# Attention and experts in one kernel: the start's order re-laid, and a dense ring of six units with a lag of five

## What is computed

```python
x = x + tanh(g_xattn) * attended(layernorm(x), ctx)   # q = ln(x) Wq + bq, k = ctx Wk + bk, v = ctx Wv + bv
h = relu(einsum('bsd,edh->ebsh', layernorm(x), W1) + b1)          # 8 experts, 512 hidden
expert_out = einsum('ebsh,ehd->ebsd', h, W2) + b2
x = x + tanh(g_ffn) * einsum('bse,ebsd->bsd', top2_weights, expert_out)
```

## Time and profile before

| | us |
|---|---|
| three runs of the kernel | 282.55, 282.98, 285.04 (median 282.98) |
| the profiled execution | 281.82 |
| its span in the profile | 280.1 |
| TensorE busy in the span | 268.3 |
| VectorE busy | 210.6 |
| ScalarE busy | 186.6 |
| GpSimd busy | 109.6 |

### The profile page before, as it was taken

The page is one execution under the profiler, slowest core; times in us unless marked ns, Lnnn a source line. Parts: engine busy times, 40 slices in busy tenths (PEclk is TensorE's granted clock), DMA queues, the critical chain, the costliest instruction groups (busy, mean ns, idle before and its releaser), DMA issues.

```text
span 280.1 us, 5068 instructions
## 1 busy us (share of the span) xinstructions
PE 268.3 (96%) x1662; PEld 246.6 (88%) x1662; DVE 210.6 (75%) x406; ACT 186.6 (67%) x338; POOL 109.6 (39%) x144
## 2 busy tenths in 40 slices
PE   7899999999999999999999999989999999994994
PEld 6678999999999999999899999978989989993994
DVE  4889977995686997898456688667797895643796
ACT  3996565446566556556579888797457557965891
POOL 3899993556600030000006346710153434375130
PEclk9999999999999999999999999999999999999898
DMA  6700020000199000000000342443011112141112
GB/s 199 255 2 0 4 76 0 2 1 2 42 292 276 1 2 0 0 4 1 0 2 4 84 140 63 148 148 103 19 32 28 30 30 67 49 114 28 60 47 84
DMA packets 18485, 17.08 MB, mean 61 GB/s; under 512 B 2410, under 2 KB 14940, under 8 KB 18460
## 3 DMA queue, kind: packets, MB, share of 16 engines
q1 hardware_dynamic: 17372, 15.31, 18.0%
q0 software_dynamic: 640, 1.31, 1.6%
q10 hardware_dynamic: 448, 0.14, 0.2%
HBM read 13.34 MB, written 3.42 MB: 60 GB/s over the span
## 4 chain that ended last, share of the span: by engine, by line
PE 84%; DVE 8%; issue 4%; DMA 2%; ACT 1%; SPq 1%; DVEq 0%; another core or an unknown queue 0%; ACTq 0%
PE ps L1448 8%; PE ps L1474 8%; PE ps L1449 8%; PE ps L1476 8%; PE ps L1475 8%; PE ps L1450 7%; PE ps L1370 7%; PE ps L1575 4%; PE ps L1561 3%; PE ps L1602 2%; DVE pmax L975 2%; PE ps L1641 2%; PE ps L1600 2%; PE ps L1643 2%; PE ps L1642 2%
## 5 line engine op out<-in xcount | busy, mean ns | idle before, releaser
L882 ACT ACTIVATE ex_hi<-ps 128x768 fp32r<-128x768 f32 (+1 forms) x78 | 56.9, 730 | 57.7 <-PE ps L1450 54.4
L1190 DVE TENSOR_TENSOR ex_lo<-ps,ex_hi 128x768 fp32r<-128x768 f32 (+1 forms) x66 | 58.5, 886 | 24.5 <-ACT ps L886 18.8
L975 DVE TENSOR_REDUCE pmax<-ps 128x1 f32<-128x512 f32 (+2 forms) x74 | 62.4, 875 | 10.2 <-PE ps L1370 9.5
L1474 PE MATMUL ps<-ex_hi,ctx_both 128*97 128x384 f32 (+1 forms) x153 | 49.8, 325 | 0.0
L886 ACT ACTIVATE ps<-ps 128x768 f32<-128x768 f32 (+1 forms) x66 | 49.7, 752 | 0.0
L1449 PE MATMUL ps<-q_lo,ctxT_hi 96*128 96x384 f32 (+1 forms) x153 | 49.1, 321 | 0.0
L1450 PE MATMUL ps<-q_hi,ctxT_lo 96*128 96x384 f32 (+1 forms) x153 | 48.7, 318 | 0.0
L1476 PE MATMUL ps<-ex_lo,ctx_both 128*97 128x384 f32 (+1 forms) x153 | 48.6, 318 | 0.0
L1475 PE MATMUL ps<-ex_hi,ctx_both 128*96 128x384 f32 (+1 forms) x153 | 48.6, 318 | 0.0
L1448 PE MATMUL ps<-q_hi,ctxT_hi 97*128 97x384 f32 (+1 forms) x126 | 42.6, 338 | 1.5 <-DVE ex_lo L1190 1.4
L1370 PE MATMUL ps<-ctxT_hi,q_hi 97*128 97x512 f32 (+1 forms) x104 | 34.3, 400 | 0.6 <-DVE pmax L975 0.4
(11 more groups left out here) (227 smaller groups left out, 547.3 us busy)
## 6 DMA issues: line engine op xcount, KB each, us to landing
raw<-in_ctx_dram SPq DMA_DIRECT2D x6, 384.0 KB, 6.4
w_raw<-in_L_ffn_W_dram SPq DMA_DIRECT2D x8, 256.0 KB, 3.9
raw<-in_L_ffn_W_dram SPq DMA_DIRECT2D x8, 256.0 KB, 6.3
raw<-in_L_ffn_b_dram SPq DMA_DIRECT2D x8, 256.0 KB
shared<-routing SPq DMA_DIRECT2D x8, 192.0 KB
x_slots<-shared SPq DMA_DIRECT2D x1, 1088.0 KB, 6.3
y_slots<-shared SPq DMA_DIRECT2D x17, 64.0 KB, 1.5
shared<-in_L_ffn_b_dram SPq DMA_DIRECT2D x1, 512.0 KB, 3.8
```

The lines of the kernel that those rows point to most:

```text
L882: nc.scalar.activation(ex_pair(ex_hi, u % P_RING, js, n), scores, ACT.Exp)
L975: nc.vector.tensor_reduce(pmax[:, FIRST_TILE[ROUND_BLOCK[r]] + t, place:place + 1], max_home(s)[:, 0:w], AX.X, ALU.max).then_inc(max_reduc ...
L1190: nc.vector.tensor_tensor(ex_pair(ex_lo, u % P_RING, js, n), whole, ex_pair(ex_hi, u % P_RING, js, n).bitcast(F32), ALU.subtract).then_inc ...
L1474: nc.tensor.matmul(dst[0:CA, :], ch[:, j, :], hi, start=(j == first), stop=False)
```

## The change

It does these things:

- Ahead of block 0, TensorE's order becomes pass, window, pass, window: pass s is followed by window s + 2. Six of the multiplications of ident with ident are left out.
- x of block 1 is no longer turned in the start. It is turned at unit 6, its queries are made at unit 8 and split at unit 9; for block 2 these are units 15, 17 and 18. A wait on rows_copied is added ahead of block 2's, since both now use the last PSUM bank.
- VectorE makes the statistics of blocks 1 and 2 at units 3 and 10, and GpSimd's power and normalizing for them move behind the split of window 6 and behind all splits of the context.
- One pass moves from unit 10 to unit 14.
- H_LAG becomes 5 and H_RING 6, with two more PSUM banks (7 and 6) and six places in the buffers, and the waits that these need. scale_output of an expert moves two units back, to the second unit of the expert after next, and the transposes of the sum move to the last rounds of the loop.

```diff
-H_LAG = 3
-H_RING = 4
+H_LAG = 5
+H_RING = 6
-WARM_NORM = 6
-    FIRST_BLOCK_PASSES = [0, 1, 1, 0, 1, 1, 1, 1, 1, 1, 1, 0, 1, 1, 1, 2, 2, 2, 2, 2, 2, 2, 2, 1, 0, 0]
+    FIRST_BLOCK_PASSES = [0, 1, 1, 0, 1, 1, 1, 1, 1, 1, 0, 0, 1, 1, 2, 2, 2, 2, 2, 2, 2, 2, 2, 1, 0, 0]
-        QK_UNIT = {1: 1, 2: 8}
-        TURN_X_UNIT = {2: 6}
-        SPLIT_UNIT = {1: 2, 2: 9}
+        QK_UNIT = {1: 8, 2: 17}
+        TURN_X_UNIT = {1: 6, 2: 15}
+        STATISTICS_UNIT = {1: 3, 2: 10}
+        SPLIT_UNIT = {1: 9, 2: 18}
-            return [UB[0], ps[:, TURNED_BY_VECTOR % 4, :], UB[1]][b]
+            return UB[1] if b else UB[0]
-            return ps[:, [3, 2, 1, 0][u % 4], :]
+            return ps[:, [3, 2, 1, 0, 7, 6][u % H_RING], :]
-        HID_AT = [2 * H, 2 * H + SPAN, 2 * H + 2 * SPAN, H]
+        HID_AT = [SPAN * k for k in (3, 4, 5, 2, 1, 0)]
...
-            inverse_deviation(1)
-            normalize(1)
...
-            inverse_deviation(2)
-            normalize(2)
             for w in range(4, 7):
                 split_ctxT(w)
+            inverse_deviation(1)
+            normalize(1)
             split_ctx(2)
...
             for g in range(3, NG):
                 split_ctx(g)
+            inverse_deviation(2)
+            normalize(2)
...
-            copy_x(1)
...
-                elif u == H_RING - 1:
-                    act.wait_ge(ys_made, SLOT_TILES - 1)
+                elif u >= 3:
+                    act.wait_ge(ys_made, SLOT_TILES)
...
-            dve.wait_ge(x_later_in, 16)
-            statistics(0, 1)
-            statistics(0, 2)
...
+                    for later, unit in STATISTICS_UNIT.items():
+                        if b == 0 and i == unit:
+                            dve.wait_ge(x_later_in, 16)
+                            statistics(0, later)
...
-                if u == FU - 1:
-                    scale_output(e - 1)
-                if u % HC == H_LAG and e > 0 and u < FU - 1:
-                    scale_output(e - 1)
+                if u % HC == (H_LAG + HC) % HC and e > 1:
+                    scale_output(e - 2)
...
+            scale_output(E - 2)
...
-            keep_warm(WARM_NORM, MPAIR[:, 0, :])
-                    pe.wait_ge(q_lo_ready, NB)
+                    pe.wait_ge(q_lo_ready, 2)
-            for w in range(2, 4):
-                turn_window(w)
             for s in range(SLOTS_UNTIL[0]):
                 score_for_max(s)
-                w = 4 + s
-                if s % 2 and w < TURNED_BY_VECTOR:
-                    turn_window(w - 1)
-                    turn_window(w)
-            turn_window(TURNED_BY_VECTOR - 1)
-            pe.wait_ge(ctxT_f_ready, TURNED_BY_VECTOR - 3)
-            turn_x(0, 1, x_home(1))
-            for w in range(TURNED_BY_VECTOR, NW - 2):
+                turn_window(s + 2)
+            for w in range(SLOTS_UNTIL[0] + 2, NW - 2):
                 turn_window(w)
...
+                        if unit > ROWS_UNIT:
+                            pe.wait_ge(rows_copied, 1)
-                    pe.wait_ge(x_copied, 2)
...
+                elif u == 4:
+                    pe.wait_ge(xs_lo_ready, SLOT_TILES)
+                elif u == 5:
+                    pe.wait_ge(r_copied, 1)
                 else:
-                    pe.wait_ge(h_lo_ready, u - 3)
+                    pe.wait_ge(h_lo_ready, u - H_RING + 1)
...
-                if v == FU - 1:
+                if v == FU + H_LAG - 2:
+                    pe.wait_ge(h_lo_ready, FU)
                     turn_sum(E - 2, UB[1])
...
-                expert_out(v - H_LAG)
+                if v >= H_LAG:
+                    expert_out(v - H_LAG)
```

More of the change, by code:

```diff
@@ L475, in ex_pair @@
             return buf[:, slot, 0:len(chunks) * n].rearrange("p (k n) -> p k n", n=n)
-        HID_AT = [2 * H, 2 * H + SPAN, 2 * H + 2 * SPAN, H]
-        assert H_RING == 4 and SPAN <= H and 2 * H + 3 * SPAN <= P_RING * 2 * MAXN
+        HID_AT = [SPAN * k for k in (3, 4, 5, 2, 1, 0)]
+        assert H_RING == 6 and SPAN <= H and 2 * H <= 3 * SPAN and 6 * SPAN <= P_RING * 2 * MAXN
         def hid(buf, u):
```

## The result

| | before | after |
|---|---|---|
| runs of the kernel, median (us) | 282.77 | 291.6 |
| ratio, with its 95% interval | | 1.029 [1.022, 1.036] |
| the profiled execution | 281.82 | 290.45 |
| its span | 280.1 | 288.7 |
| first exponential starts | 19.73 | 20.78 |

The times are medians of all executions, while the ratios and their intervals leave out executions more than 1.5% above the fastest of their kernel, so a ratio is not the quotient of the medians beside it.

The account below looks back on a forecast made before the run. TensorE, busy 96% of the span, was taken as the bound. The terms 1.67 + 0.90 + 1.2 + 0.8 - 1.6 gave +3.0 us, put on the timed median for 286.0 us, range 281.4 to 288.6.

Parts of the forecast that it names:

- first windows: Start: windows turned behind the passes slow the loop and delay the first exponential, +1.67 us, bounds -0.9 and +2.2.
- work moved into the full stretch: First attention block, where TensorE has no idle time: block 1's x transposes (0.25) and queries (0.65) move in, +0.90 us.
- wait at unit 6: TensorE waits before block 1's x transposes for late statistics, power and normalizing: +1.2 us, bounds 0 and 2.4.
- wait at unit 12: TensorE's scores wait for the second row of maxima, behind block 2's statistics: +0.8 us, bounds 0 and 1.2.
- dense layers: Dense layers at the end: a lag of five covers part of ScalarE's pauses, -1.6 us, bounds 0 and -5.5.
- pairs: Start: pairs of passes, fed by ScalarE's roundings of turned windows, start 2.8 us apart in place of 2.1.
- Rival C: The start isn't slower: VectorE's maxima start 0.9 us earlier and decide the entry; 281.4 us, chance 0.17.
- the dense hole: TensorE's late second layers at units 14 and 15 plus low clock, 5.5 us before; one hole of 2 to 3 stays.
- Rival D: Dense layers: the ring gives nothing, as pauses follow the gathers and TensorE idles the same; 287.6 us, chance 0.15.
- the reading by place in the program: Dense layers: if pauses belong to places in ScalarE's program, they return at the same units; gain about 1.8 us.

Follow-up runs that it names:

- e5: The changed kernel unedited, run again for its trace where ScalarE pauses: 288.93 against 281.72 us for the kernel before, 1.0204.
- e7: The changed kernel with the windows in the order of before, two ahead of each two passes: 288.67 against 281.72 us, 1.0215.
- e10: The changed kernel with the edits of e3, e7 and e9 at once: 276.16 against 274.29 us for the kernel before, 1.0099.
- e9: The kernel before with the ring of six, lag of five and scale_output one unit earlier, where ScalarE makes no pauses: ratio 0.9996.
- e4: The changed kernel with block 2's addition of EPS made by GpSimd instead of VectorE: 279.98 against 274.03 us, 1.022.
- e14: The changed kernel unedited, run beside e13 on a chip without pauses: 282.03 against 274.22 us for the kernel before, 1.0283.
- e2: The kernel before with the ring of six and lag of five alone, without pauses: 274.73 against 274.03 us, 1.0025.
- e15: Repeat of e2, the kernel before with the deeper ring alone, where ScalarE makes no pauses: ratio 1.0023.
- e17: Repeat of e2, the kernel before with the deeper ring alone, where ScalarE pauses: ratio 1.0014 to the kernel before at 282.15 us.
- e1: The changed kernel with the dense layers of the kernel before (ring of four, lag of three): 281.32 against 274.03 us, 1.0247.
- e11: The changed kernel with the six matmuls of ident put back: 283.81 against 274.29 us for the kernel before, 1.0332.
- e18: The kernel before with the ring of six, lag of five and scale_output one unit earlier, where ScalarE pauses: ratio 0.9914.
- e13: The changed kernel with 15 useless matmuls of ident in TensorE's hole ahead of unit 12's scores: 279.92 us, 1.0207 to the kernel before.
- e3: The changed kernel with block 2's statistics moved behind the second row of maxima (unit 11 instead of 10): 278.37 against 274.03 us, 1.0161.
- e8: The changed kernel with block 1's statistics at unit 1 and block 2's at unit 11: 285.85 against 281.72 us, 1.0124.

## Why the prediction was wrong, by its steps

The direction was right, the size was not. In the profile after, +5.78 are made by block 1's first scores, where the forecast had +4.57; +2.11 between there and the dense layers, where it had nothing; and +0.70 in the dense layers, where it had -1.6. By the terms of the sum, with what the runs put in their place:

| term | forecast | measured | from |
|---|---|---|---|
| first windows | +1.67 | +1.05 to +1.55 | first exponential: after, e5 against e7 |
| work moved into the full stretch | +0.90 | +0.93, and 0.6 unassigned | e10 against e9 |
| wait at unit 6 | +1.2 | +0.76 | idle in after 0.78, in e10 0.76 |
| wait at unit 12 | +0.8 | +2.14, of which 1.45 the addition's wait | idle in after, e4 has 0.48 |
| low clock behind unit 12 | none | 0 to 4.4 in profiles, 0.8 on average in e14 | unit 12 to block 1; e14's runs |
| block 2's attention | none | +2.11 in after, none in e5 | profiles |
| dense layers | -1.6 | +0.7 in after; ring alone +0.6 to +0.7 without pauses, about 0 with | profile after; e2, e15, e17 |

**First windows.** The mechanism held: pairs 2.76 us apart where 2.8 were forecast, and e7 undoes the delay of the first exponential. The term was high by 0.1 to 0.6, and the first exponential (20.78) came just ahead of the forecast 21 to 22. Rival C fell: the first maximum starts 0.9 us earlier in after (9.42), as C had it, and the first exponential is late all the same.

**Moved work.** Right in size, but for the 0.6 that stays unassigned. The queries cost what they were priced at: where they stood they left a gap of 0.65 at the third unit's scores.

**Unit 6.** Right in kind and within its bounds. **Unit 12** is the first step that failed: "the statistics of block 2 stand before the row and take 1.14", and the bounds ended at 1.2. The durations came from 7.68 to 9.95 in the earlier trace rows, where GpSimd had little to do. In after the same instructions take 2.68 (42.31 to 44.99), since the addition waits for GpSimd's subtraction. Without the 1.45 of that wait the idle would have been 0.69, near the forecast 0.8: the place and the order were right, the addition's duration was not.

**The clock** is the second step that failed. The prediction spoke of the clock only for the dense hole. It forecast two holes of about 1 us in the first block and gave neither a price beyond its length. After's own profile has no low clock at unit 12, so its +5.78 at block 1 is holes and work alone; the profiles of e1, e7, e11 and e14 have some. After's profile lost 2.1 more in block 2, by ScalarE's pause there (1.25 idle became 1.91) and the low clock behind. e5 has the same pause at 1.28 without the fall, and e17, with before's start, has an idle of 2.00 and the fall: that part is not the change's but the execution's.

**The dense layers** are the third step that failed, and in the profile after the largest miss (2.3). "A lag of five runs two first layers further ahead" is what the trace shows, and the idle before unit 15's second layer is 1.41, not 2.94. But the prediction priced the waits that the ring adds and left out the one that it moves: scale_output for an expert now stands behind ex_lo of the second unit of the expert after next, which VectorE can't make until ScalarE's pause is over, and TensorE needs it for y_bank at unit 16. Rival D came out, for another reason than it gave. With scale_output a unit earlier the time falls by 1.9 where there are pauses (e18), near the forecast -1.6, but in part by luck. The forecast kept the low clock behind the hole and took its gain out of idle time; in e18 the idle before units 15 and 16 is 1.59 + 1.48 = 3.07, in before's profile 0.91 + 2.94 = 3.85, so 0.8 less, and the clock that stayed full makes much of the rest.

That the pauses keep to ScalarE's units 13 to 16, wherever in time the dense layers lie, speaks for the reading by place in the program; that three chips don't have them no run explains.

## What to carry to other kernels

A forecast hole on the full engine has two prices, its length and what the clock does behind it; where it can't be closed, filling it with harmless matmuls was cheap here and made the times even (e13). A short VectorE operation on numbers in SBUF must not be priced from a row in which GpSimd was idle if it moves beside GpSimd's long ones; and where it heads a queue that TensorE waits for, it belongs on GpSimd or behind the urgent one. When a ring is deepened, follow each buffer that isn't in the ring (here y_bank and its scale_output) and ask whether its release now stands behind the thing the ring was to cover.

## What the runs showed of the hardware that was not expected

- VectorE's addition on 128x3 numbers took 0.17 us with GpSimd idle and 1.62 beside a subtraction of 1.66 that had started 0.06 earlier (after; 1.62 in e5 and 1.61 in e14). Statistics (e3) and the row of maxima, which has an operand in PSUM (e4), were not delayed beside it.
- After the same idle of 2.12 to 2.14 us the granted clock stayed at full speed (after, e5) or fell to 0.50 for stretches that cost 1.5 (e7), 3.0 (e1) and 4.4 us (e11), worked out from unit 12 to block 1: 31.05 us without low clock, 32.56, 34.00 and 35.48 with it. With the idle cut to 0.52 it didn't fall (e13).
- In e8 TensorE came to its full clock at 14.1 us of the span, in the other 19 profiles at 4.7 to 7.5, and the first exponential came 3 us late (23.90; after: 20.78).
- The same kernel takes 274 us on some chips and 282 on others. Of the 8, about 6 are ScalarE's pauses in the dense layers with the low clock behind them, and 1.3 one in block 2; the matmuls themselves step alike.
